# A four-layer sequence kernel: the second experts' scatters add onto the stream in memory, a plain copy makes the output, and the index columns are used in place

## The reference, cut to what matters

```
x = x + linear_attention(layernorm(x))          # 16 heads
x = x + experts0(layernorm(x))                  # 8 experts, top 2 by softmax, silu(x w1) * (x w3) @ w2, hidden 256
x = x + hyperbolic_attention(layernorm(x))      # 16 heads, softmax over 2048 keys
x = x + experts1(layernorm(x))                  # 8 experts, the 2 farthest centroids, hidden 684, with biases

def experts(xs):                                # what both mixtures compute
    out = 0
    for e in range(8):
        out = out + weight[:, e] * (h_e(xs) @ W2[e] + b2[e])
```

## Time and profile before

| what | value |
|---|---|
| median of 3 runs (2408.89 to 2412.17) | 2411.94 us |
| the profiled execution's own time | 2414.36 us |
| its span | 2412.6 us |
| mean granted clock of TensorE | 0.938 |
| busy: PE, PEld, DVE, ACT, POOL | 2079.7, 971.6, 1389.4, 1534.8, 440.3 us |
| DMA | 220.11 MB, mean 91 GB/s |
| 142 gathers (L982) | mean 1019 ns of POOL |
| 142 scatters (L988) | mean 988 ns of POOL |
| second experts' weights: `halves`, `w2halves`, each of 8 experts | 1368 KB and 684 KB |
| first experts, first gather to last scatter | 263.1 to 517.0 us |
| second experts, the same | 1905.2 to 2371.0 us |
| last stage, first load to the end of the span | 2376.3 to 2412.6 us |

### The profile page before, as it was taken

The page is one execution under the profiler, slowest core; times in us unless marked ns, Lnnn a source line. Parts: engine busy times, 40 slices in busy tenths (PEclk is TensorE's granted clock), DMA queues, the critical chain, the costliest instruction groups (busy, mean ns, idle before and its releaser), DMA issues. The chain is left out here.

```text
span 2412.6 us, 43912 instructions
## 1 busy us (share of the span) xinstructions
PE 2079.7 (86%) x13329; PEld 971.6 (40%) x13330; DVE 1389.4 (58%) x2986; ACT 1534.8 (64%) x2495; POOL 440.3 (18%) x678
## 2 busy tenths in 40 slices
PE   5997799950996999999999999999853699999992
PEld 4785455530661222222222222222242476766761
DVE  5567444347786444444445555553156687777774
ACT  2215333223774999999999999999862344444441
POOL 0030366642000000000000000000000134343430
PEclk9998899975996999999999999999976799999996
DMA  5001344443100000000002222222255265555656
GB/s 194 1 1 70 105 148 146 142 144 140 38 24 1 1 1 1 1 1 1 1 19 71 71 71 71 71 71 71 83 180 164 98 178 175 173 176 170 175 168 231
DMA packets 139075, 220.11 MB, mean 91 GB/s; under 512 B 14080, under 2 KB 108464, under 8 KB 138944
## 3 DMA queue, kind: packets, MB, share of 16 engines
q1 hardware_dynamic: 124160, 176.96, 23.6%
q0 software_dynamic: 13632, 37.24, 4.7%
q10 hardware_dynamic: 1152, 4.19, 0.4%
HBM read 161.82 MB, written 52.20 MB: 89 GB/s over the span
## 5 line engine op out<-in xcount | busy, mean ns | idle before, releaser
L1800 ACT ACTIVATE at_pexp<-at_psS 128x1024 f32<-128x1024 f32 x1024 | 964.2, 1023 | 42.9 <-PE at_psS L1706 39.8
L1814 DVE TENSOR_REDUCE at_mx<-at_psM 128x1 f32<-128x512 f32 x474 | 327.5, 691 | 464.3 <-PE at_psM L1733 464.3
L1720 PE MATMUL at_psO<-at_pexp,at_vst 128*32 128x512 f32 x4096 | 546.4, 605 | 0.1
L1706 PE MATMUL at_psS<-l1c_QT,l1c_KT 64*128 64x512 f16 x2048 | 403.6, 387 | 14.4 <-issue 5.6
L1706 PEld LDWEIGHTS at_psS<-l1c_QT,l1c_KT 64*128 64x128 f16 x2048 | 99.4, 92 | 632.4 <-ACT at_pexp L1800 598.9
L2136 PE MATMUL ex_psH<-wide_wgu,ex_xT 128*128 x1278 | 259.9, 357 | 0.2 <-issue 0.2
L2207 DVE SCALAR_TENSOR_TENSOR ex_bias<-ex_psH,top_w_scale,ex_bias 128x456 f32<-128x456 f32 x213 | 147.4, 692 | 76.7 <-PE ex_psH L2136 63.8
L988 POOL DMA_INDIRECT expert_rows<-ex_y,ex_odx x142 | 140.3, 988 | 259.5 <-issue 181.3
L2180 ACT ACTIVATE ex_sg<-ex_bias 128x228 f32<-128x228 f32 x213 | 83.7, 393 | 152.1 <-DVE ex_bias L2207 152.1
L1733 PE MATMUL at_psM<-at_ksumT,l1c_QT 64*128 64x512 bf16 x474 | 179.1, 378 | 0.6
L2136 PEld LDWEIGHTS ex_psH<-wide_wgu,ex_xT 128*128 128x128 f16 x1278 | 124.5, 97 | 111.8 <-issue 3.6
(11 more groups left out here) (362 smaller groups left out, 2782.6 us busy)
## 6 DMA issues: line engine op xcount, KB each, us to landing
ex_bias<-in_L_ffn_bg SPq DMA_DIRECT2D x71, 342.0 KB
ex_bias<-in_L_ffn_b SPq DMA_DIRECT2D x71, 342.0 KB
ex_piece<-in_L_ffn_W SPq DMA_DIRECT2D x48, 228.0 KB, 2.6
l1c_KT<-in_L_ffn_W SPq DMA_DIRECT2D x32, 342.0 KB, 3.4
halves<-l1c_KT SPq DMA_DIRECT2D x32, 342.0 KB, 3.3
wide_wgu<-halves SPq DMA_DIRECT2D x8, 1368.0 KB
ex_b<-in_L_ffn_b SPq DMA_DIRECT2D x71, 128.0 KB
normed<-rt_area SPq DMA_DIRECT2D x16, 512.0 KB, 2.6
```

Source lines behind the costliest of these rows:

```text
L1706: mm = pe.matmul(psS[:, n, hh * BANK:(hh + 1) * BANK], keys(k.KT, p)[r, kt * P:(kt + 1) * P], keys(k.QT, p)[r, c * BANK:(c + 1) * BANK], s ...
L1720: mm = pe.matmul(psO[g * VW:(g + 1) * VW, y, :], vst[:, p % 2, hh, kt, :], pexp[:, (p * ST + step) % 3 * 2 + n, hh * BANK:(hh + 1) * BANK] ...
L1800: act.activation(pexp[:, u % 6, :], psS[:, u % 2, :], ACT.Exp, scale=D ** -0.5 / (QS * QS)).then_inc(raised, 1)
L1814: dve.tensor_reduce(mx[:, n:n + 1], psM[:, :], AX.X, ALU.max).then_inc(reduced, 1)
```

## The change

In `slot_transfers` both loops over tiles are written out in full, the copies L968 and L973 go with their buffers and the semaphores `indexed` and `passed`, and gather and scatter take the columns of `k.tok` and `k.dst` themselves as indices. In the first experts PE reads both expert numbers at the top of a step, before the transposes.

For the second mixture both rows of a token are the same row of a new DRAM tensor `sums`, to which the routing stage has stored the stream; the scatters add to it, each after the one before has landed. The last stage is four copies from `sums` to the output, two on SP's queue and two on ACT's. Five experts' weights instead of four are loaded in `attention_out`, three in the routing, with the nine stores behind them (eight of 512 KB, one of 256 KB). The loads of the first two tiles' biases wait until those tiles' gathers have landed.

```diff
@@ route @@
+    rows = T if layer else 2 * T
...
-                ser(dve.tensor_scalar(dstv[:, :, 1], row[:, :], float(T), None, ALU.add))
+                ser(dve.tensor_scalar(dstv[:, :, 1], row[:, :], float(rows - T), None, ALU.add))
...
-                ser(dve.tensor_scalar(pad[:, :], pad[:, :], float(2 * T + 1), -1.0, ALU.mult, ALU.add))
+                ser(dve.tensor_scalar(pad[:, :], pad[:, :], float(rows + 1), -1.0, ALU.mult, ALU.add))
@@ slot_transfers @@
-    for st in steps(pool, NTILE, 8, LAG):
...
+    for at in range(NTILE + LAG):
+        if at < NTILE:
+            t, g = at, at % GR
+            if t >= GR:
+                pool.wait_ge(got[g], t // GR * 16)
+                pool.wait_ge(x_turned, t - GR + 1)
             pool.indirect_dma_start(xg[:, g, :], None, k.xn_d,
-                                    bass.IndirectOffsetOnAxis(idx[:, g, :], 0)).then_inc(got[g], 16)
...
+                                    bass.IndirectOffsetOnAxis(k.tok[:, t:t + 1].bitcast(U32), 0)).then_inc(got[g], 16)
+        if at >= LAG:
+            t, j = at - LAG, at % 2
+            if t >= 2:
+                pool.wait_ge(put[j], t // 2 * 16)
+            where = bass.IndirectOffsetOnAxis(k.dst[:, t:t + 1].bitcast(U32), 0)
+            if sums is None:
+                pool.wait_ge(y_done, t + 1)
+                pool.indirect_dma_start(k.y_d, where, y[:, j, :], None).then_inc(put[j], 16)
+            else:
+                if t:
+                    pool.wait_ge(put[1 - j], (t + 1) // 2 * 16)
+                else:
+                    pool.wait_ge(k.sums_in, 16 * (NT // 4 + 1))
+                pool.wait_ge(y_done, t + 1)
+                pool.indirect_dma_start(sums, where, y[:, j, :], None, compute_op=ALU.add).then_inc(put[j], 16)
@@ experts0, PE @@
                 for st in steps(pe, NTILE, 8, 3):
+                    eh, ey = (pe.value_load(k.tile_expert[0:1, ds(st.tile(lag), 1)], min_val=0, max_val=E - 1)
+                              if st.on(lag) else None for lag in (1, 3))
...
-                        e = pe.value_load(k.tile_expert[0:1, ds(t, 1)], min_val=0, max_val=E - 1)
@@ combine -> copy_sums @@
+        to = out.rearrange("b (p g t) c -> g p b (t c)", p=P, g=G)
+        rows = k.sum_d[0:T, :].rearrange("(p b g t) c -> g p b (t c)", p=P, b=NB, g=G)
...
+                for g in range(0, G, 2):
+                    sp.dma_start(to[g], rows[g]).then_inc(out_sem, 16)
+                sp.wait_ge(out_sem, 16 * G)
...
+                for g in range(1, G, 2):
+                    act.dma_start(to[g], rows[g]).then_inc(out_sem, 16)
+                act.wait_ge(out_sem, 16 * G)
@@ new @@
+def store_sums(sp, k):
+    G = 4
+    rows = k.sum_d[0:T, :].rearrange("(p t) c -> p t c", p=P)
+    for g in range(NT // G):
+        sp.dma_start(rows[:, g * G:(g + 1) * G, :], k.x[:, g * G:(g + 1) * G, :]).then_inc(k.sums_in, 16)
+    sp.dma_start(k.sum_d[T:T + 2 * P, :].rearrange("(p t) c -> p t c", p=P), k.x[:, 0:2, :]).then_inc(k.sums_in, 16)
@@ experts1, SP @@
                         e = sp.value_load(k.tile_expert[0:1, ds(t, 1)], min_val=0, max_val=E - 1)
+                        if isinstance(t, int) and t < BR:
+                            sp.wait_ge(got[t], 16)
@@ program @@
+        def rest(sp):
+            load_experts(sp, k, a, range(EARLY, E))
+            store_sums(sp, k)
+        EARLY = E // 2 + 1
+        attention_out(nc, k, lambda sp: load_experts(sp, k, a, range(EARLY)))
+        route(nc, k, "rt1", 1, k.cent, k.x, rest)
         experts1(nc, k, a)
-        combine(nc, k, "cb1", out.rearrange("b (p t) c -> p b t c", p=P))
+        copy_sums(nc, k, "cb1", out)
```

More of the change, by code:

```diff
@@ L954, in _, with slot_transfers @@
                 ser(dve.tensor_scalar(k.tok[:, :], k.dst[:, :], T - 1, None, ALU.bitwise_and))
-def slot_transfers(pool, k, idx, odx, xg, y, got, put, x_turned, y_done, indexed, passed):
+def slot_transfers(pool, k, xg, y, got, put, x_turned, y_done, sums=None):
     LAG = GR + 2
-    for st in steps(pool, NTILE, 8, LAG):
[L963 to L981, removed]
-            pool.indirect_dma_start(xg[:, g, :], None, k.xn_d,
-                                    bass.IndirectOffsetOnAxis(idx[:, g, :], 0)).then_inc(got[g], 16)
[L984 to L989, removed]
@@ L1011, in experts0 @@
         got, put = s.sems("got", GR), s.sems("put", 2)
-        indexed, passed = s.sem("indexed"), s.sem("passed")
         AR = 4
@@ L1039, in _ @@
             def _(pool):
-                slot_transfers(pool, k, idx, odx, xg, y, got, put, x_turned, y_done, indexed, passed)
+                slot_transfers(pool, k, xg, y, got, put, x_turned, y_done)
             @block.tensor
@@ L1149, in _ @@
             def _(sp):
[L1150 to L1165, removed]
+                for g in range(0, G, 2):
+                    sp.dma_start(to[g], rows[g]).then_inc(out_sem, 16)
+                sp.wait_ge(out_sem, 16 * G)
             @block.scalar
             def _(act):
-                for g in range(NT // G):
-                    act.wait_ge(added, g + 1)
-                    bb, t0 = g * G // TB, g * G % TB
-                    act.dma_start(x_out_dram[:, bb, t0:t0 + G, :], k.x[:, g * G:(g + 1) * G, :]).then_inc(out_sem, 16)
-                act.wait_ge(out_sem, 16 * (NT // G))
+                for g in range(1, G, 2):
+                    act.dma_start(to[g], rows[g]).then_inc(out_sem, 16)
+                act.wait_ge(out_sem, 16 * G)
 def combine_and_log_map(nc, k):
@@ L2091, in _ @@
             def _(pool):
-                slot_transfers(pool, k, idx, odx, xg, y, got, put, x_turned, y_done, indexed, passed)
+                slot_transfers(pool, k, xg, y, got, put, x_turned, y_done, k.sum_d)
             @block.sync
@@ L2256, in program @@
         k.x2_d = nc.dram_tensor("stream", [T, C], F32).ap()
+        k.sum_d = nc.dram_tensor("sums", [T + 2 * P, C], F32).ap()
         k.wgu_src = [a["L1_ffn_Wg"], a["L1_ffn_W1"], a["L1_ffn_W2"]]
```

19 lines of the change are left out of this document (5 added, 14 removed).

## The result

The changed kernel takes **2377.12 us** (median of 4 runs, 2375.96 to 2377.97) against 2411.18 for the kernel before (4 runs, 2408.89 to 2412.17): 34.1 us less, a ratio of 0.986 with a 95% interval of 0.9843 to 0.9877. The forecast was 2372.0 in a range of 2358 to 2396. The time is 5 us above the forecast, and the terms behind it were off by more than that, in both directions. The profiled execution took 2376.76 us with a span of 2375.0, close to the median.

The account below looks back on a forecast made before the run. It took POOL to bound the first experts, PE the second, and transfers the last stage. Terms 17.1 + 1.3 + 6.0 - 2.0 + 17.8 = 40.2 from 2411.9 gave 2372 us, range 2358 to 2396.

Parts of the forecast that it names:

- POOL bound the first experts, PE the second: Both expert stages before the change: POOL sets 3.40 us a tile in the first, PE 6.31 in the second.
- First experts, forecast 18.4: First expert stage: index columns in place gain 17.1 us over 61 tiles, plus 1.3 at first gather and last scatter.
- I take 3.12, its quickest in the loop that stays: First experts: PE, next limit after POOL, goes from 3.40 to 3.12 us a tile, gaining 17.1 us.
- The reads on PE, forecast zero: First experts: both expert-number reads at the top of PE's step cost nothing; bounds zero and 0.28 us a tile.
- the rival's 0.3 to 0.6: First experts: PE's two reads together leave this bubble in us each tile, so PE stays at 3.40; 2389 us, chance 0.17.
- fourth rival: First experts: transfers with indices in place keep the 0.8 us gap, 3.58 us a tile; 2401 us, chance 0.03.
- Start of the second experts, forecast 6.0: Second experts' start: earlier gather, with bias loads waiting for it, gains 6.0 us; bounds 3 and 6.5.
- The serial wait in the middle, forecast zero: Second experts, steady part: the adding scatters' chain turns in 3.8 us, hidden behind PE's 6.31 a tile.
- second rival: Second experts: adding scatters landing after 5.5 us or more make POOL set the pace; about 2480 us, chance 0.06.
- The end, forecast -2.0: Second experts' last scatters: serial wait shows, costing 2.0 us at landing 3.0; 0.3 at 2.4, 9.2 at 5.4.
- Moved transfers, at nothing: Expert loads and nine stores moved to the attention's output and routing cost nothing, covered by DVE's arithmetic there.
- Last stage, forecast 17.8: Last stage of 36.3 us becomes copies taking 18.5, middle of 13 (bytes counted once) and 23 (twice); gain 17.8.

Follow-up runs that it names:

- experiment 2: Kernel before with only the index columns in place and POOL's list written out, in both mixtures; 2399.07 us, ratio 0.9947.
- experiment 5: Changed kernel with PE's list of the first experts written out for all 74 steps instead of a register loop; 2367.26 us, ratio 0.9826.
- experiment 6: Kernel before the change with PE's list of the first experts written out and nothing else; 2410.53 us, ratio 1.0.
- experiment 4: Changed kernel without the wait of the first two tiles' bias loads on the gathers; 2379.48 us, ratio 0.9869.
- experiment 10: Changed kernel with PE's first-experts list written out and the four copies issued inside the second experts' stage; 2365.72 us, ratio 0.9814.
- experiment 9: Changed kernel with four experts' weights loaded in the attention's output and four in the routing, as before the change; 2377.77 us, ratio 0.9856.
- experiment 7: Changed kernel whose last stage also copies the sums to a scratch tensor first, 4.19 MB more; 2391.28 us, ratio 0.9917.
- experiment 3: Changed kernel whose second experts' scatters write without adding, still one after the other; 2372.37 us, ratio 0.9844.
- experiment 8: Changed kernel without the last stage: SP and ACT issue the four copies inside the second experts' stage; 2373.03 us, ratio 0.9837.
- experiment 1: Changed kernel with PE reading each expert number right before its use again, not at the top of the step; 2380.31 us, ratio 0.987.

## Why the forecast was right, and where its terms were not

**POOL bound the first experts, PE the second: shown.** With the copies gone POOL waits for DVE, the stage is 12 us shorter, and experiments 2, 5 and 6 give the order of the limits: POOL 3.40, PE's loop 3.24, and 3.12 with PE's list written out and PE busy 159.8 of 160 us.

**First experts, forecast 18.4, measured 12.35.** The step that failed is "I take 3.12, its quickest in the loop that stays". An engine bound by its own loop goes at the mean of a turn, and the quickest interval is one of eight. The true next limit was 3.24; with it the term would have been 61 x (3.40 - 3.24) + 1.3 = 11.1. The 3.02 of the first tiles was no pace of the steady part at all: experiment 5, with every step written out, has it at the same first tiles too and goes at 3.12 behind them. What makes those tiles quicker is open.

**The reads on PE, forecast zero, measured a gain of about 2.** The text said that the traces have no row for PE's read. That was wrong: they have, on PE's sequencer. Of the changed kernel:

```profile
L1043 PEldq FUSED_REGOPS  x205: 37/151/165, 270.7 to 502.1; - x103
L1043 PEldq TENSOR_LOAD <-top_tile_expert x142: 295/301/497, 270.1 to 501.8; - x142
```

The load itself takes 0.30 us, but each has register work behind it, and from the first load's start to the end of the second's work it is 1.3 to 1.4 us at every step from 300 to 400. So the rival's 0.3 to 0.6 beyond the 1.03 us of L1077 was about right, and what held is the forecast's argument against it: L1069 is queued too. SP's 0.79 was the whole distance between two issues, not the read. The Trainium skill ("DMA: Bandwidth & Descriptors", Latency and other measured facts) has a floor of some 600 ns for such a load. Here it takes half of that; the measurement decides. Idle time put down to issue ahead of L1051 was 2.6 us in 8 times from 290 to 480, and nearly none in experiment 5 (0.2).

**The gap of 0.8 (fourth rival): not there.** It is 0.30 ahead of a gather that nothing held back.

**Start of the second experts, forecast 6.0.** Behind the first gather it came to 6.36 for 5.3, and the early landing was the mechanism named. PE turned the first tile 2.9 us behind its gather (3.1 forecast), and L2129 started 2.1 later (2.4). DVE's first bias addition was held by the bias load, at 9.37 us behind the gather where the forecast had 8.3 (1912.8 less 1904.5): 1.1 late. The step that failed is the weight given to this addition. The stage follows PE's first L2129: it starts 5.04 us behind the gather for 11.15 before, 6.1 sooner, and from there to DVE's last y it is 451.6 us for 451.8. The view I formed after the result, that the two bias waits do next to nothing (0 to 2 us), made the same mistake and fell with experiment 4.

**The serial wait in the middle, forecast zero: right.** 6.307 us a tile with and without the addition. At the end of the stage the scatters' chain turns in 1.55 + 2.82 = 4.37 us, a landing of 3.65 and 0.72 until the next start (0.78 in the forecast), so 1.9 us a tile are left there before the second rival would have begun. That margin isn't safe: in experiment 10's trace the median landing is 5.6 us, at the rival's threshold of 5.5, and DVE waits for scatters.

**The end, forecast -2.0, measured -5.25.** The step that failed is "I take 3.0, as both sides of the transfer are under way together". The last three scatters land after 3.63, 3.65 and 3.73 us. The forecast's own line from 0.3 at 2.4 through 9.2 at 5.4 rises 3 us per us of landing and gives 0.3 + 3 x 1.3 = 4.2 there. Up to the last landing the loss is 3.9, so this part of the mechanism was right and its size was off. The other 1.4 is a term that the forecast didn't have: POOL's DRAIN behind the last scatter, 4.29 us for 2.92. The Trainium skill says that such a transfer reads its destination and writes it later ("DMA: Bandwidth & Descriptors", Rules for kernel authors). The direction agrees, as the last landing is 1.3 us longer than a plain one's, but no run separates the read from the write. The full sum of both, 5.4, it is not.

**Moved transfers, at nothing: right** (experiment 9).

**Last stage, forecast 17.8, measured 20.0.** The stage took 16.3, between the two readings of 13 and 23, nearer the first. The term mis-sized is "I take the middle, 18.5", and neither of the readings holds (experiment 7). By the Trainium skill's 207 to 214 GB/s per direction ("DMA: Bandwidth & Descriptors", Latency and other measured facts) an estimate is 22; the stage moved 336 GB/s with full engines, and at the margin 296 (experiment 7). The measurement decides; the tiles behind the Trainium skill's figure had 16 KiB in each partition, the rows here 4 KB.

**The sum.** The terms off by -6.0, -3.3, +2.2 and +1.1 make -6.0, and by the medians the gain was 34.1 for 40.2, which is that. The profiled execution lost only 2.6 of it, since the stretch between the expert stages gave some back. That stretch is the one row of the account that no edit explains. Of the profiled kernels whose code there is the changed kernel's, six (after and experiments 3, 5, 7, 8 and 10) have it at 1380.8 to 1386.2, and two (experiments 1 and 4, whose profiled executions were also their slowest) at 1390.9 and 1389.3; the kernels with the old code (before, 2 and 6) have it at 1389.2, 1385.9 and 1388.0. The bands overlap, and within them the routing alone varies by 4 us. So 5 us of that stretch can't be read as a gain, and a stage's gain has to be read inside the stage. That the total came within 6 us is in part luck, as the terms missed by 12.6 us in all, in both directions.

## What to carry to other kernels

When one engine stops being the bound, the next limit is the mean over a whole turn of the other's loop, not its quickest interval; and its sequencer's rows (reads, register operations) belong to that reading. Writing out the list of the engine that becomes the bound is then worth trying, and worth nothing before. A serial chain of transfers that hides in the steady part shows once at the end, at the price of its landing and of POOL's DRAIN behind it. Transfers that follow can be issued in the stage that makes their data and save the block's end (4.1 us here alone, 1.5 on top of experiment 5). Where a stage is bound by PE, look at when PE's first matmuls start, not at the first wait of another engine.

## What was not expected of the hardware

- An indirect scatter that adds takes POOL 1.59 us where a plain one of the same 128 rows of 1 KB takes 0.99. Beside the bias loads it lands after 4.0 us for 3.5 (medians), at the end of the stage after 3.7 for 2.4. In one execution of experiment 10 the median was 5.6.
- POOL's DRAIN at the end of a stage takes 4.29 us when its last scatters add and 2.91 or 2.92 when they don't, in every trace here.
- A copy within the memory runs at 336 GB/s with the DMA engines full, loads and stores of the old last stage at 401 with the engines equally full, both in packets of 4 KB.
- Four bias loads of 342 KB issued beside it make PE wait 6.1 to 8.65 us for a gather instead of 2.9 to 3.1 (four traces against eight).
- Two executions of the same code between the expert stages differ by up to 10 us in the traces (1380.8 to 1390.9), while the four medians of the kernel before lie within 1 us (2410.75 to 2411.72).
